# Two small GpSimd additions, each waited for, ahead of every row scatter of a two-layer attention and mixture-of-experts kernel

## The reference

```
x = x + xattn0(layernorm(x), ctx)      # 16 heads of 8, masked
x = x + moe0(layernorm(x))             # top 2 of 8 experts, silu, 512 wide
x = x + xattn1(layernorm(x), ctx)      # rope, window of 64
x = x + moe1(layernorm(x))             # top 2 of 8 gated experts, 176 wide, and a shared one
```

## Time and profile before

| | |
|---|---|
| time, three runs | 694.60, 695.43, 695.74 us; median 695.43 |
| profiled execution, span from the first to the last instruction | 763.9 us |
| time of the profiled execution outside its span | not shown |
| TensorE busy | 671.5 us, 88% of the span |
| VectorE busy | 523.5 us, 69% |
| GpSimd busy | 504.9 us, 66% |
| ScalarE busy | 415.8 us, 54% |
| scatters on line 626 | 128, 126.9 us busy |
| granted TensorE clock, mean of the span | 0.953 of full speed |

### The profile page before, as it was taken

One profiled execution on the slowest core, in us unless ns is written; L12 is line 12 of the kernel. 1 busy time (PEld: TensorE's weight loads), 2 busy tenths in 40 slices (PEclk: granted clock), 3 DMA queues, 4 the chain that ended last, 5 costly groups with the idle time before them and its releaser, 6 DMA issues.

```text
span 763.9 us, 21054 instructions
## 1 busy us (share of the span) xinstructions
PE 671.5 (88%) x7092; PEld 546.5 (72%) x7092; DVE 523.5 (69%) x1515; ACT 415.8 (54%) x1158; POOL 504.9 (66%) x837
## 2 busy tenths in 40 slices
PE   8799998888876999999979999888888668788797
PEld 7567666665646999999957776666667568778787
DVE  5489988888663446555358898888886555555556
ACT  5477767654542434444447777656547445555563
POOL 5975788577564678877677778777667635455451
PEclk9899999999997999999979999999989989899999
DMA  5470000001331522343110101111211312222264
GB/s 166 124 305 2 17 27 27 27 30 36 137 99 48 160 70 81 97 127 89 46 36 29 30 26 40 54 37 37 66 34 37 89 51 77 61 75 72 75 232 152
DMA packets 45406, 57.78 MB, mean 76 GB/s; under 512 B 11379, under 2 KB 37142, under 8 KB 44630
## 3 DMA queue, kind: packets, MB, share of 16 engines
q1 hardware_dynamic: 36086, 38.17, 16.6%
q0 software_dynamic: 8640, 17.97, 7.1%
q10 hardware_dynamic: 576, 0.29, 0.1%
HBM read 33.82 MB, written 22.08 MB: 73 GB/s over the span
## 4 chain that ended last, share of the span: by engine, by line
PE 50%; POOL 17%; issue 12%; DVE 8%; ACT 5%; another core or an unknown queue 4%; DMA 2%; SPq 1%; DVEq 0%; POOLq 0%; ACTq 0%
POOL results L1625 9%; PE ptp L1349 8%; PE M L1366 7%; PE ptp L2078 6%; PE S L1326 5%; PE S L2059 5%; PE S L1330 3%; PE ptp L1352 3%; POOL xi L1618 2%; POOL rows L626 2%; PE M L1374 2%; PE M L1418 2%; PE S L2065 1%; SPq L707 1%
## 5 line engine op out<-in xcount | busy, mean ns | idle before, releaser
L626 POOL DMA_INDIRECT rows<-out_rows,posi x128 | 126.9, 991 | 50.1 <-issue 32.1
L806 ACT ACTIVATE pT<-ptp 128x512 f32<-128x512 f32 (+1 forms) x192 | 95.1, 525 | 97.7 <-PE ptp L1349 87.0
L1929 POOL DMA_INDIRECT results<-early,xs x71 | 69.0, 971 | 68.4 <-DVE early L2001 50.9
L1064 DVE TENSOR_REDUCE mx<-S 128x16 f32<-128x1232 f32 x64 | 91.3, 1427 | 18.3 <-PE S L1330 16.4
L1625 POOL DMA_INDIRECT results<-early,xi x71 | 75.9, 1069 | 40.5 <-DVE early L1687 35.1
L1065 DVE TENSOR_TENSOR pr<-S,mx 128x1232 f32<-128x1232 f32 x64 | 92.3, 1442 | 2.2
L1724 PE MATMUL S<-first_w,early 128*128 x568 | 77.2, 279 | 3.0 <-DVE early L1687 1.5
L1714 PE MATMUL S<-early,w1s 128*128 128x128 f32 x568 | 76.9, 279 | 0.6 <-ACT early L1659 0.6
L1366 PE MATMUL M<-pT,vm 128*32 128x128 f32 (+1 forms) x2048 | 74.7, 283 | 1.1 <-ACT pT L806 0.6
L1349 PE MATMUL ptp<-cst,pr 128*128 128x128 f32 x512 | 74.0, 290 | 0.0
L1724 PEld LDWEIGHTS S<-first_w,early 128*128 128x128 f32 x568 | 69.5, 193 | 5.9 <-issue 5.7
(11 more groups left out here) (221 smaller groups left out, 1527.9 us busy)
## 6 DMA issues: line engine op xcount, KB each, us to landing
xs<-rows SPq DMA_DIRECT2D x142, 66.0 KB
first_w<-in_e_W SPq DMA_DIRECT2D x2, 2048.0 KB, 8.2
swap<-results SPq DMA_DIRECT2D x32, 128.0 KB
first_w<-results SPq DMA_DIRECT2D x6, 512.0 KB
rows<-out_rows,posi POOLq DMA_INDIRECT x128
x_res<-in_x SPq DMA_DIRECT2D x1, 1536.0 KB, 8.4
W1r<-in_e_W SPq DMA_DIRECT2D x1, 1536.0 KB, 10.8
out_x<-x_res SPq DMA_DIRECT2D x3, 512.0 KB, 2.7
```

What stands on the lines that cost most here:

```text
L626: nc.gpsimd.indirect_dma_start(rows[:, :], bass.IndirectOffsetOnAxis(posi[:, k, n:n + 1], 0), out_rows[:, ring_slot(groups, n), k, :], Non ...
L806: nc.scalar.activation(pT[0:rows_of, G * r:G * r + count, :], ptp[q % 2][0:rows_of, 0:count, :], ACT.Exp, scale=SCALE)\
L1064: do(V.tensor_reduce(mx[:, :].rearrange("p (g j) -> p g j", g=G), sc, AX.X, ALU.max))
```

## The change

In front of each of the two DMAs of `scatter`, a new function `pause` issues two additions of one column on GpSimd, `zero + zero` as unsigned 32-bit integers, into a new tile `paused` of 128x1, which nothing reads. Each addition is followed by a wait of GpSimd for its completion. Both layers call it; 256 additions and 256 waits are added in all, and nothing is removed or moved.

```diff
             for k in range(2):
+                pause()
                 nc.gpsimd.indirect_dma_start(rows[:, :], bass.IndirectOffsetOnAxis(posi[:, k, n:n + 1], 0),
                                              out_rows[:, ring_slot(groups, n), k, :], None).then_inc(scattered[lane(groups, g)], 16)
+
+        def pause():
+
+            for _ in range(2):
+                steps.then(pool, nc.gpsimd.tensor_tensor(st["paused"][:, 0:1], zero[:, 0:1], zero[:, 0:1], ALU.add))
...
+        st["paused"] = sb("paused", [128, 1], U32)
```

## The result

The changed kernel takes 738.5 us (median of four runs, 734.8 to 741.2) against 695.6 us of the kernel before in four runs on the same chip: a ratio of 1.061 [1.057, 1.065], +42.9 us. The forecast was 756 us, with a range of 705 to 792: slower, as foretold, by 43 us in place of 61.

The account below looks back on a forecast made before the run. GpSimd was taken as full, or level with what paces the loop, early in attention 0, with waits later; 13.7 + 16.6 + 31.1 + 3 = 64.4 us on the profile's span, taken as 61: 695.4 + 61 = 756 us, range 705 to 792.

Parts of the forecast that it names:

- GpSimd paces both loops "or is level with what does": Attention 0, 86.05 to 130.09 us: GpSimd full, its waits for other engines only 1.5 us of 44.
- The rival of the waits that stay: Attention loops: GpSimd's waits are loop latencies and don't shrink, so nothing is deducted; +97, 792 us; chance 5%.
- the rival of 691 us: Experts 0 and 1: pauses thin out piled-up scatters, up to 15.5 us of ScalarE's standstill come back; not slower; chance 4%.
- What one pause costs: GpSimd, ahead of each of 128 scatters: four pieces giving 0.95 us for each scatter, 122 us in all.
- Addition, wait, scatter: GpSimd, last wait of a pause: scatter starts 0.78 us behind the addition, taken from line 614.
- The prediction's own sign of being wrong: Profile after, GpSimd ahead of a scatter: gap staying at 0.17 to 0.3 us instead of about 0.78.
- The rival of late integer additions: GpSimd's pauses: the 0.78 also stands between the two additions; +152 us, 847 us; chance 10%.
- What reaches the end: Both attentions and tails: each stretch grows by added time less GpSimd's waits in it; 64.4 us on the profile's span.
- The short start rival: Scatters start 0.17 us behind the pause, about 0.41 us cost each; +11 us, 707 us; chance 17%.
- The waits' cover in the tails: Scatters after each attention loop: GpSimd's waits cover layer 0's 11.4 us fully; layer 1's leave +3 us.

Follow-up runs that it names:

- the second profile of before: The kernel before, profiled once more with no edit: profiled span 695.5 us, timed 697.2 against 697.3 us.
- experiments 8 and 9: Kernel before, no pause, waits for `pos_ready` and `idx_set` ahead of a group's first scatter swapped: 693.3 against 697.3 us; on another chip 693.6 against 697.7.
- the tails alone: Kernel before plus pauses only for scatters behind the last step (12 in layer 0, 18 in layer 1): 700.8 against 697.0 us.
- the early index: Kernel before with the index addition issued ahead of line 584 of its step and the two waits swapped: 697.7 against 697.7 us.

## Why the prediction was right, and where not

**GpSimd paces both loops "or is level with what does": right, in the weaker form.** GpSimd paces them after the change: its waits for others are gone from the first loop, and its share of the chain there is 73%. Before the change it is level with VectorE, which has the larger share of the chain (62% against 17% in the first loop). Both results fit that: added time counts almost in full, and time taken off gains little. In the profile that the prediction read, the chain from 84 to 212 us is 81% TensorE and 1.5% GpSimd; it asked GpSimd's waits alone and didn't look at the chain. The effect is additive over the layers (21.0 + 21.6), and the dose is regular: 12.0, 42.9 and 105.5 us for one, two and four additions, and -4 us for half a microsecond less at some group starts. The rival of the waits that stay (792 us) is out, as GpSimd's waits went. So is the rival of 691 us. Its mark, ScalarE's 7.8 and 7.7 us for an unnamed queue, is no trait of the kernel: in the second profile of before no releaser of that kind is left in the chain, where the first had 4%.

**What one pause costs: two pieces right, one wrong.** The addition (0.20) and the second one behind a wait (0.28 start to start) came out. The step that failed is "Addition, wait, scatter: line 614 ends at 127.00, and the scatter, which waits for it, starts at 127.78, a gap of 0.78": the gap is 0.28. The bill is 0.44 us per scatter, near the low end of 0.41, not 0.95. I had a warning in my own text ("one pattern, with two semaphores on the DMA") and still took its whole size for that of a wait. By the groups of experiments 8 and 9, 0.78 is the way of the semaphore that is waited for second of two, and a pause leaves the scatter a single one. The prediction's own sign of being wrong, a gap that "stays at 0.17 to 0.3", is what the trace shows, and the eight steps from the third scatter on take 6.1 us each (5.1 before) where it had 7.2. The rival of late integer additions is out too: the additions stand 0.08 apart.

**What reaches the end: the rule right, its waits wrong.** "A stretch grows by the added time less GpSimd's waits in it" holds once the waits are those of a usual execution. A scatter's +0.44 and about 0.02 at the handover behind it are 0.46. Layer 0: 50 x 0.46 = 23.0, less 3.9 = 19.1, measured 19.5. Layer 1: 46 x 0.46 = 21.2, less 6.8 (six waits of 0.6 to 2.2 us for line 1366 and before `norms` in the second profile) = 14.4, measured 16.0. My sum deducted 17.2 and 12.6 for the same stretches, from the earlier trace rows. This second error pulled down what the first had pulled up: with the right price and the wrong waits, the loops would have given 7.4 - 1.5 = 5.9, then 15.6 - 15.7, none, and 21.2 - 12.6 = 8.6, together 15 us and not 35.5. The short start rival, which had nearly the right price, said +11 us for that reason. The forecast is nearer than either because its two errors have opposite signs: that it came within 18 us is luck.

**The waits' cover in the tails: right in kind.** Layer 0's tail costs nothing, as said (12 x 0.46 = 5.5 us against waits of 3.6 and 6.05). Layer 1's was given 3 us "late for the first result, and behind its landing the load of tile 16"; that chain is what the rows show, with 4.9 us up to the first result and +3.8 us for the tails alone. From the first result to the end, another 110.4 - 108.3 = 2.1 us were lost. Whether that belongs to the tile loads or to TensorE's clock (1.00 before, 0.95 after in that stretch) I didn't separate.

**The ledger**, from the second profile of before to the one after: +0.6 before layer 0's loop; the loop +19.5; its tail and experts 0, with 5.5 us of pauses in them, -1.6, which makes 18.5 at layer 1's first scatters (435.48 to 453.93, window starts); layer 1's loop +16.0; its tail +4.9; experts 1 +2.1: 41.5 us between the spans of 695.5 and 737.0.

**The range held**, but not by its reasoning: 738.5 lies between the short start with the first profile's waits (707) and the forecast, a place that no case of the prediction describes.

**Open:** why the semaphore that is waited for second has the longer way to the DMA, what makes the five groups that don't fit, why one addition ahead of the group's first scatter leaves the start at 0.81 behind line 614, why the early index gained nothing in the timed runs, and what made the first profiled execution slow.

## What to carry to other kernels

Before reading slack from a profiled execution, compare its span with the timed runs; if it is 10% longer, durations can still be used, but its waits can't, and a second profile comes before any sum. Take the price of a wait from a place with one semaphore and the same two kinds of instruction; a gap with two causes is an upper bound, not a price. Look at the chain in the stretch as well as at one engine's waits. And where an engine has next to no waits in a loop that others need it for, half a microsecond a piece counts almost in full, though its busy share over the whole kernel is 73%, and the cheapest thing to try there is the order of its waits. In these traces the DMA starts soonest when the semaphore that comes last is waited for first. What is gained that way ends where the next engine is full, here VectorE.

## What the runs showed of the hardware that I had not expected

- The same kernel, profiled twice, had spans of 763.9 and 695.5 us, with busy times within 0.3% on GpSimd, VectorE and ScalarE. TensorE's busy time was 671.5 against 645.2 us at a mean granted clock of 0.953 against 0.973; the rest of the difference lies in waits.
- On GpSimd, a wait for its own operation just issued costs 0.14 us ahead of an addition and 0.11 ahead of an indirect DMA. The indirect DMA needs 0.17 us behind an operation without a wait and 0.30 behind another indirect DMA.
- An indirect DMA on GpSimd that waits for two semaphores starts 0.28 us behind the end of what raises the one waited for first, and 0.78 to 0.81 behind what raises the second, whichever is later (19 of 20 groups before, 16 of 20 with the swapped waits). With a small waited addition between, it starts 0.81 after line 614's end. The Trainium skill ("DMA: Bandwidth & Descriptors", Anatomy of one DMA) gives about 50 ns for a dispatch from GpSimd. None of these gaps is that short, the shortest is 0.15; how much of a gap is the dispatch, no run here shows.
